# Decoder layer on one core: how the decay factors of the gated delta rule are made, and where some key, gate and selection work stands

## The chip, the cores and the metric

One core of a Trainium2 chip runs the whole layer as one program. The metric is the device time of one launch in microseconds (us). Five engines run their own instruction streams and meet at semaphores: PE (TensorE, matmuls), DVE (VectorE), ACT (ScalarE), POOL (GpSimd) and SP (SyncE, which here only issues DMAs). All arithmetic is in 32-bit floats, so the trace shows several PE records for each matmul.

## The reference

The input is x (4 x 256 x 256) and a context (4 x 256 x 64). Three things follow each other: a linear attention with state (gated delta rule with two keys and values per token, 8 heads of width 128), a mix of its output by a top-k mask over similarities of the context, and a feed-forward part with 8 routed experts. The change touches the first, and the order of the selection that belongs to the second:

```
q = conv_silu(x @ Wq), k = conv_silu(x @ Wk), v = conv_silu(x @ Wv)   (two k, v per token)
q = l2norm(q) / sqrt(Dh),  k = l2norm(k),  beta = 2 sigmoid(x @ Wb)
g = -exp(A_log) * softplus(x @ Wa + dt_bias)                           (one per token and head)
per token:  state *= exp(g);  for j in 0, 1:
                u = (v_j - k_j . state) * beta_j;  state += k_j (x) u
            o = q . state
out = (rmsnorm(o) * norm_w * silu(x @ Wg)) @ Wo
```

The kernel works through it in chunks of 64 tokens (4 per sequence, 16 in all). Within a chunk it needs, for each pair of positions, exp of a sum of g between them; across chunks exp of the sum from the start and to the end.

## The kernel before

**Steps and stages.** `run_heads` runs 11 steps (0 to 10). In step s head s is in stage A, head s-1 in B, s-2 in C and s-3 in E, so four heads are worked on side by side. Each engine has its own program with the same step loop, and each step has a place `FIRST`, slots 0 to 11 and a place `LAST`. The table `FILL` says which extra piece ("item") of which stage stands in which place; PE fills a PSUM bank with it, and another engine empties the bank. Items share three banks in rotation (`bank_of`), so PE waits for the item three before.

- Stage A: ten projections (`proj`, line 582) in slots 0 to 9 through two banks; ACT copies each with the last filter tap (`evac`, line 833), DVE adds the other three taps (`conv`, line 1055), ACT applies silu (line 857) and squares; PE sums the squares (`norm`, line 611), DVE takes them over (`norm_sum`, lines 1083 to 1091) and folds them into beta (`fold_beta`, lines 1100 to 1105).
- The decay factors of head A: POOL multiplies g by a mask of "upto" (`gm`, line 1287), PE sums it over tokens in the items `dx` and `ex` (line 596, four products of 64 x 128 x 512), ACT takes exp of each bank (line 872, after a load of the table for exp, line 866). POOL masks dx into `dm` (line 1308), later multiplies dx by minus beta (line 1315), then makes `kn` (line 1296), copies scalars and multiplies q by ex into `qE` (line 1337).
- Stage B: the items `pair` at `FIRST` (eight, line 637), which DVE empties with two products into `aT` and `mq` (lines 1121 and 1126); then the inverse of the triangular 128 x 128 matrices. For it SP writes the diagonal 32 x 32 blocks of `aT` to memory (line 445) and reads them back turned so that a block lies in a partition (`blk`, line 448), POOL solves them in 62 dependent operations (`invert`, lines 1370 and 1373), SP writes and reads back the result (lines 454 and 459, the last as four DMAs into `TT`), DVE transposes it (`turn_blocks`, slot 9, line 1144), and PE combines it in the items p32 (line 663), t32 (667), x32 (669), p64 (671) and t64 (673) with ACT copies between them. `vtok` and `kend` (line 639) are transposes of v and k; DVE scales kend (line 1132). `gate` (line 590) are the gate products, which ACT passes through silu.
- Stage C is the scan over the chunks (lines 683, 697, 711, 712, 716). After it ACT squares the output (`out_square`, line 889) and DVE makes `og` (line 1197). Stage E is the output projection `out` (line 746).

**Order.** It is written out by hand: each engine goes through its instructions in program order, and so does SP's queue. In a step SP issues gather (`a_blocks`, `blk`), the loads of weights, a tile of similarities, and scatter (the inverses). In step 1 it then writes out the similarities (`tiles_out`, line 425) and waits for them; POOL waits for the same before it clears `TT` of head 1. POOL's order in a step is: clear and unit of the inverse (lines 1347, 1354, 1358), cwh and gm, the factor of stage E, invert, dm, fold, kn, scalars, qE. DVE also works on the top-k selection: `topk` runs 20 operations for each tile, 8 in slot 0 and 12 in slot 11.

After the steps the feed-forward part follows, which the change doesn't touch.

## Time and profile before

| what | value |
|---|---|
| median of 3 runs | 939.75 us (938.98 to 943.63) |
| the profiled execution's own time | 943.89 us |
| its span, from first to last instruction | 941.8 us |
| PE busy | 834.6 us (89%) |
| DVE busy | 527.5 us (56%) |
| ACT busy | 393.7 us (42%) |
| POOL busy | 346.9 us (37%) |
| mean granted TensorE clock | 0.942 of 2.4 GHz |

The steps can be told in the trace by the eight pair items (line 637) with which each begins on PE: steps 1 to 8 begin at 55.0, 120.5, 187.8, 255, 320.8, 386.4, 453.7 and 519.7 us. DVE's transpose into X (line 1144) ends at 108.0, 170.8, 373.0 and 572.4 us in steps 1, 2, 5 and 8, and SP's first gather DMA of step 2 is issued at 123.8. The feed-forward part is from 625 us to the end. Within one engine rows that follow each other are merged; "[x <- y]" is idle time ahead of the row and what ended it.

### The profile page before, as it was taken

The numbers are of one execution on the slowest core, as the hardware profiler recorded it, in microseconds if no ns is written. First come the engines' busy times: TensorE is split into PE (matmuls) and PEld (weight loads), VectorE is DVE, ScalarE is ACT, GpSimd is POOL, SyncE is SP. The second block draws the span as 40 slices with busy tenths as digits, with TensorE's granted clock in tenths as the row PEclk, the third lists the DMA queues.
The fourth block names the chain that finished last, engine by engine and source line by source line (L and its number), as shares of the span: only waits on it lengthen the run. The fifth ranks groups of instructions, "written<-read, shape, count | busy, mean of one in ns | idle before, by whom it ended". The sixth has DMA issues, their size and how long they took to land.

```text
span 941.8 us, 16248 instructions
## 1 busy us (share of the span) xinstructions
PE 834.6 (89%) x5560; PEld 582.0 (62%) x5561; DVE 527.5 (56%) x1283; ACT 393.7 (42%) x843; POOL 346.9 (37%) x654
## 2 busy tenths in 40 slices
PE   3759999989999999899899766867999999999992
PEld 2334576766766766667667755755666667666761
DVE  4655668678878878878888763564411111111113
ACT  3637765455654565555565332113222222222220
POOL 0158358437456564573584470003420000000015
PEclk9978999799999999999999975985999999999997
DMA  8320330030031021121201301019563101110104
GB/s 203 79 59 9 74 79 13 13 79 12 13 79 23 9 73 23 35 46 24 51 2 24 90 3 26 1 33 377 194 238 111 33 22 33 33 33 22 33 24 127
DMA packets 102594, 57.88 MB, mean 61 GB/s; under 512 B 64192, under 2 KB 98048, under 8 KB 102528
## 3 DMA queue, kind: packets, MB, share of 16 engines
q1 hardware_dynamic: 99488, 51.62, 20.4%
q0 software_dynamic: 1536, 4.20, 1.5%
q10 hardware_dynamic: 1504, 1.20, 0.4%
q8 instruction: 39, 0.64, 0.3%
q14 instruction: 27, 0.22, 0.1%
HBM read 42.45 MB, written 14.55 MB: 61 GB/s over the span
## 4 chain that ended last, share of the span: by engine, by line
PE 70%; DVE 7%; POOL 7%; ACT 6%; issue 5%; DMA 4%; SPq 1%; POOLq 0%; ACTq 0%; DVEq 0%
PE bank L1600 16%; PE bank L582 11%; PE bank L1645 9%; PE bank L590 3%; PE bank L637 3%; PE bank L746 3%; DVE y L1055 3%; PE bank L712 2%; POOL inv L1373 2%; POOL term L1370 2%; PE bank L1632 2%; PE bank L711 2%; PE bank L697 2%; PE bank L596 2%; PE bank L671 2%
## 5 line engine op out<-in xcount | busy, mean ns | idle before, releaser
L1055 DVE SCALAR_TENSOR_TENSOR y<-bank,cwh,y 128x510 f32<-128x510 f32 (+2 forms) x240 | 177.5, 743 | 77.1 <-ACT y L833 73.4
L582 PE MATMUL bank<-xnT,wbuf 128*128 128x512 f32 x320 | 159.8, 624 | 7.4 <-DVE y L1055 6.8
L1600 PE MATMUL bank<-f_wgu,f_xgT 128*128 x368 | 118.8, 466 | 0.0
L1878 DVE TENSOR_TENSOR f_act<-f_sg,bank 128x352 f32<-128x352 f32 x62 | 32.2, 521 | 144.3 <-PE bank L1600 142.0
L1370 POOL TENSOR_TENSOR term<-inv,blk 128x126 f32<-128x126 f32 (+22 forms) x248 | 87.4, 352 | 62.8 <-DMA blk<-a_blocks 44.0
L1953 POOL DMA_INDIRECT f_back<-slots_y,f_slot x16 | 15.4, 960 | 231.5 <-DMA slots_y<-f_yb 224.9
L1373 POOL TENSOR_TENSOR inv<-inv,term 128x126 f32<-128x126 f32 (+22 forms) x248 | 91.1, 367 | 19.4
L582 PEld LDWEIGHTS bank<-xnT,wbuf 128*128 128x128 f32 x320 | 55.6, 193 | 66.2 <-issue 50.8
L1717 ACT ACTIVATE f_sg<-bank 128x352 f32<-128x352 f32 x62 | 28.6, 463 | 161.7 <-PE bank L1600 153.3
L1645 PE MATMUL bank<-f_wdn,f_actT 128*128 (+1 forms) x372 | 91.5, 388 | 0.9 <-ACT f_actT L1730 0.8
L1600 PEld LDWEIGHTS bank<-f_wgu,f_xgT 128*128 128x128 f32 x368 | 66.2, 190 | 36.8 <-issue 7.6
L833 ACT ACTIVATE y<-bank,cwh 128x512 f32<-128x512 f32 x80 | 54.9, 686 | 71.2 <-PE bank L582 69.3
L1645 PEld LDWEIGHTS bank<-f_wdn,f_actT 128*128 128x128 f32 x372 | 67.9, 189 | 24.5 <-issue 12.0
L1315 POOL TENSOR_TENSOR dx<-dx,minus_beta 128x1024 f32<-128x1024 f32 x8 | 15.2, 1902 | 114.6 <-DVE beta_n L1105 114.6
L637 PE MATMUL bank<-kq 128*128 128x192 f32 x256 | 46.3, 336 | 8.0 <-DVE mq L1126 8.0
L712 PE MATMUL bank<-mq,R 128*128 128x64 f32 x256 | 48.0, 286 | 3.1 <-DVE R L1162 3.1
L932 ACT ACTIVATE vtok<-bank,kn 128x128 f32<-128x128 f32 x128 | 36.4, 369 | 30.1 <-PE bank L642 30.1
L637 PEld LDWEIGHTS bank<-kq 128*128 128x128 f32 x256 | 42.2, 193 | 10.6 <-DVE mq L1126 9.8
L1300 POOL TENSOR_TENSOR factor<-factor,masks 128x8 f32<-128x8 f32 x8 | 13.3, 1662 | 88.8 <-DVE factor L1206 88.8
L1600 PE MATMUL bank<-f_wgu,f_x2T 128*128 128x352 f32 x128 | 45.5, 503 | 0.4 <-DVE f_act L1878 0.4
L712 PEld LDWEIGHTS bank<-mq,R 128*128 128x128 f32 x256 | 39.9, 203 | 6.6 <-DVE R L1162 3.7
L596 PE MATMUL bank<-gm,masks 64*128 64x512 f32 x64 | 27.5, 686 | 14.6 <-ACT dx L872 8.0
(206 smaller groups left out, 1511.7 us busy)
## 6 DMA issues: line engine op xcount, KB each, us to landing
f_wgu<-in_exp_gu SPq DMA_DIRECT2D x8, 1408.0 KB, 9.4
f_wdn<-in_exp_dn SPq DMA_DIRECT2D x8, 640.0 KB, 9.9
blk<-a_blocks SPq DMA_DIRECT2D x16, 256.0 KB, 3.8
slots_x<-oT SPq DMA_DIRECT2D x24, 128.0 KB, 1.9
f_xg<-slots_x SPq DMA_DIRECT2D x24, 128.0 KB, 2.0
slots_y<-f_yb SPq DMA_DIRECT2D x23, 128.0 KB, 1.7
a_blocks<-aT SPq DMA_DIRECT2D x64, 32.0 KB, 1.6
inverses<-inv SPq DMA_DIRECT2D x16, 128.0 KB, 3.0
```

Source lines behind the costliest of these rows:

```text
L582: last = mm(bankA[p % 2][:, :], wbuf[A.par][:, kt, wblk, :], xnT[:, kt, (p % 2) * 512:(p % 2 + 1) * 512], start=kt == 0, stop=kt == 1)
L596: return mm(bank[:, :], mask("rest" if kind == "dx" else "ones", i * STEPS, STEPS), gm[half_, :, :].rearrange("p n t -> p (n t)"), start=T ...
L637: last = mm(bank[:, c * (MU + STEPS):(c + 1) * (MU + STEPS)], kraw[:, 2 * n + c, :], kq[:, 2 * n + c, :], start=True, stop=True)
L712: last = mm(out, U[:, b, :], mq[par][:, b, c, :], start=c == 0, stop=True)
L833: a(y[p % 2][:, :, :].rearrange("p b t -> p (b t)"), bankA[p % 2][:, :], ACT.Copy, scale=cwh[A.par][:, cb, 3:4]).then_inc(evac_done, 1)
L932: last = a(vtok[B.par][:, b, c, :], bank[:, c * P:(c + 1) * P], ACT.Copy, scale=kn[:, b * CH + c:b * CH + c + 1])
L1055: v.scalar_tensor_tensor(out=y[p % 2][:, :, k:], in0=src[:, :, 0:SEQ - k], scalar=cwh[A.par][:, cb, 3 - k:4 - k], in1=y[p % 2][:, :, k:], ...
L1370: g.tensor_tensor(step_term, inv[:, 0:r, j:j + 1].to_broadcast([P, r, k]), blk[:, j:j + 1, j + 1:].to_broadcast([P, r, k]), ALU.mult).then ...
L1373: g.tensor_tensor(inv[:, 0:r, j + 1:], inv[:, 0:r, j + 1:], step_term, ALU.add).then_inc(inv_done if j == NB - 2 else inv_step, 1)
L1600: last = mm(gu[c][:, 0:FFH], xt[:, k, :], wgu[:, e, k, at:at + FFH], start=k == 0, stop=k == 1)
L1645: last = mm(dn[par][:, 0:HID], aT[0:rows, par, k, :], wdn[0:rows, e, k, :], start=k == 0, stop=k == FT - 1)
L1878: v.tensor_tensor(av[:, par, half * FFH:(half + 1) * FFH], sg[:, half, :], gu[2 * half + 1][:, 0:FFH], ALU.mult).then_inc(f_act, 1)
```

## The change

The sums of g are made once for all heads, in two small products in step 0, and kept both as columns (`g_cols`, a token pair per partition) and as rows in memory (`sums`). For each head SP loads the rows of the head into all 128 partitions, twice: into `dr` (for pairs) and into `ex`. POOL subtracts the column from the row and masks with an affine select; ACT takes exp of `dr` into `dm` and of `ex` in place, one instruction of 1024 columns each; POOL makes dx from dm and minus beta. The items dx and ex are gone from PE, and gm from POOL.

Besides: ACT scales kend (four copies with a scale) in place of DVE; kend 2 moves from slot 11 to 9, the gate products from slots 9 and `LAST` to 4 and 9; `norm(A, 5)` moves behind x32, in a new place `BLOCKS_64` ahead of `LAST`; `out_square` moves there too, ahead of p64; of the four DMAs into TT those of blocks 0 and 2 are issued first, and DVE waits for these two alone; topk is split 5, 4 and 11 operations in slots 0, 2 and 11.

```diff
 FILL = {FIRST: {"B": [("pair", n) for n in range(BC // 2)]},
-        0: {"A": [("dx", 0), ("dx", 1), ("ex", 0), ("ex", 1)]},
...
-        4: {"E": [("out", 1)]},
+        4: {"E": [("out", 1)], "B": [("gate", 0)]},
...
-        9: {"B": [("gate", 0)]},
+        9: {"B": [("kend", 2), ("gate", 1)]},
         10: {"B": [("p32", 0), ("p32", 1)], "E": [("out", 3)]},
-        11: {"B": [("t32", 0), ("t32", 1), ("kend", 2)]},
-        LAST: {"B": [("x32", 0), ("x32", 1), ("gate", 1), ("p64", 0), ("p64", 1), ("t64", 0), ("t64", 1)]}}
+        11: {"B": [("t32", 0), ("t32", 1)]},
+        BLOCKS_64: {"B": [("x32", 0), ("x32", 1)]},
+        LAST: {"B": [("p64", 0), ("p64", 1), ("t64", 0), ("t64", 1)]}}
+SCALARS_AT = 3
+EXP_AT = {0: 7, 1: 2}
```

SP's queue:

```diff
+        def rows_to(A_h, out, done):
+            for i in range(2):
+                src = halves[i][A_h * BC // 2:(A_h + 1) * BC // 2, :].rearrange("(a n) t -> a (n t)", a=1)
+                sp.dma_start(out[:, i * BC // 2:(i + 1) * BC // 2, :]..., src.to_broadcast([P, BC // 2 * STEPS])).then_inc(done, 16)
+        def difference_rows(h):
+            if h:
+                sp.wait_ge(dm_done, h)
+            rows_to(h, dr, dr_in)
+        def decay_rows(h):
+            if h:
+                sp.wait_ge(qe_done, 2 * h)
+            rows_to(h, ex, ex_in)
...
             if B:
                 gather(B)
+            if s == 1:
+                decay_rows(1)
             if A and A.h < HEADS - 1:
                 loads(A.h + 1)
...
+            if s == 0:
+                ...        (writes the rows out, waits, difference_rows(0), decay_rows(0))
+            if A and A.h < HEADS - 1:
+                difference_rows(A.h + 1)
             if B:
                 scatter(B)
+            if A and 1 <= A.h < HEADS - 1:
+                decay_rows(A.h + 1)
             if s == 1:
                 tiles_out()
                 tile_in(0)
```

ACT (per head; in steps 0 and 1 both stand in slots 7 and 2, else before slot 0 with `keep_k` between them) and POOL:

```diff
+        def decays(A):
+            nc.scalar.preload_act_table_set(LN_EXP)
+            act.wait_ge(ex_in, 32 * (A.h + 1))
+            a(ex[:, :, :], ex[:, :, :], ACT.Exp).then_inc(ex_done, 1)
+        def pair_decays(A):
+            act.wait_ge(dr_step, 2 * A.h + 2)
+            if A.h:
+                act.wait_ge(qk_used, 8 * A.h)
+            a(dm[:, :, :], dr[:, :, :], ACT.Exp).then_inc(dm_done, 1)
+        def differences(h):                                              # POOL
+            pool.wait_ge(dr_in, 32 * (h + 1))
+            g.tensor_tensor(dr, dr, g_cols[:, h, :] (broadcast), ALU.subtract).then_inc(dr_step, 1)
+            pool.wait_ge(dr_step, 2 * h + 1)
+            g.affine_select(out=dr, in_=dr, pattern=[[0, BC], [2, STEPS]], ..., fill=-1000.0).then_inc(dr_step, 1)
...
-                decays(A)
                 fold_beta(A)
                 norm(A)
                 scalars(A)
                 q_decay(A)
+                if A.h < HEADS - 1:
+                    differences(A.h + 1)
```

## Rows read from the trace of the kernel before

**Rows 1.** Busy time by stage: us, PE, PEld, DVE, ACT, POOL, PEclk, DMA share, GB/s

```profile
320.90:386.50 65.60, 62.71 (x533) 44.33 (x533) 54.49 (x127) 37.45 (x73) 38.40 (x77) 1.00 0.17 37
386.50:453.90 67.40, 64.50 (x533) 45.04 (x534) 54.60 (x127) 37.50 (x74) 38.47 (x77) 0.97 0.18 37
```

**Rows 2.** Timeline of step 5 (320 to 386 us): start us, us, engine, line

```profile
320.77 2.22 PE L637 MATMUL bank<-kq 128*128 128x192 f32 x12
324.33 3.52 PE L637 MATMUL bank<-kq 128*128 128x192 f32 x20 [1.33 <-DVE mq L1126]
334.51 0.69 ACT L833 ACTIVATE y<-bank,cwh 128x512 f32<-128x512 f32 x1 [1.32 <-PE bank L582]
371.57 1.42 DVE L1144 STREAM_TRANSPOSE X<-TT 32x512 f32<-32x512 f32 x2
373.38 1.20 PE L663 MATMUL bank<-X,aT 32*32 32x32 f32 x64
380.33 1.07 ACT L946 ACTIVATE XP<-bank 64x512 f32<-64x512 f32 x2
382.52 2.08 PE L671 MATMUL bank<-XP,aT 64*64 64x64 f32 x32
```

**Rows 3.** Groups of instructions by line: busy us, mean ns, idle before

```profile
L596 PE MATMUL bank<-gm,masks 64*128 64x512 f32 x64 | 27.5, 686 | 14.6 <-ACT dx L872 8.0 <-POOL gm L1287 6.6
L639 PE MATMUL bank<-masks,kT 128*128 128x128 f32 x96 | 16.2, 296 | 0.0
L1132 DVE TENSOR_TENSOR kend<-bank,sh 128x512 f32<-128x512 f32 x24 | 16.4, 684 | 10.5 <-PE bank L639 10.5
L932 ACT ACTIVATE vtok<-bank,kn 128x128 f32<-128x128 f32 x128 | 36.4, 369 | 30.1 <-PE bank L642 30.1
L1315 POOL TENSOR_TENSOR dx<-dx,minus_beta 128x1024 f32<-128x1024 f32 x8 | 15.2, 1902 | 114.6 <-DVE beta_n L1105 114.6
L889 ACT ACTIVATE osq<-oT 128x1024 f32<-128x1024 f32 x8 | 8.4, 1045 | 0.0
```

**Rows 4.** Chain of waits of step 2, from the last product into aT

```profile
125.99 0.44 DVE aT L1121
...
170.08 0.70 DVE X L1144
```

**Rows 5.** DVE and POOL at the ends of steps 1 and 5, and line 1358

```profile
114.49 1.01 DVE L1091 TENSOR_SCALAR qn<-turned 128x8 f32<-128x8 f32 x1
...
383.82 2.50 POOL L1337 TENSOR_TENSOR qE<-kq,ex 128x512 f32<-128x512 f32 x2
...
385.75 1.53 DVE L1091 TENSOR_SCALAR qn<-turned 128x8 f32<-128x8 f32 x1
...
388.09 1.28 DVE L1197 SCALAR_TENSOR_TENSOR og<-oT,normw,gate 128x1024 f32<-128x1024 f32 x1 [0.82 <-ACT osq L889]
389.29 0.42 DVE L1121 TENSOR_TENSOR aT<-bank,dx 128x256 f32<-128x256 f32 x1
...
L1358 POOL TENSOR_SCALAR_AFFINE_SELECT inv<-inv x16: 716/722/1772, 64.6 to 521.4; 64x512 f32<-64x512 f32 x16
```

**Rows 6.** Timeline of step 0 (ACT) and of the start of step 1 (PE)

```profile
28.10 1.28 ACT L866 ACT_TABLE_LOAD   x1 [1.47 <-PE bank L596]
...
67.52 3.75 PE L596 MATMUL bank<-gm,masks 64*128 64x512 f32 x6 [6.13 <-POOL gm L1287]
```

**Rows 7.** Timeline of step 1: SP's queue, and POOL's qE

```profile
104.19 7.71 SPq L425 DMA_DIRECT2D similarities<-TT  x4
...
118.61 2.50 POOL L1337 TENSOR_TENSOR qE<-kq,ex 128x512 f32<-128x512 f32 x2
```

**Rows 8.** Timeline of the end of step 8, and DMAs by line

```profile
584.49 3.78 PE L590 MATMUL bank<-xnT,wg 128*128 128x512 f32 x4
...
594.33 0.64 PE L725 MATMUL bank<-osq,masks 128*32 128x256 f32 x8 [1.63 <-ACT osq L889]
...
blk<-a_blocks SPq DMA_DIRECT2D x16, 256.0 KB, 3.8
```

More of the change, by code:

```diff
@@ L144, in order_table @@
         for place in PLACES:
-            for stage, items in items_at(place, step):
+            for stage, items in items_at(place):
                 if 0 <= step - LAG[stage] < HEADS:
@@ L752, in fill @@
             def fill(place):
-                for stage, items in items_at(place, number(A, B, C, E)):
+                for stage, items in items_at(place):
                     if stages[stage]:
@@ L819, in scalar_values @@
             for i in range(2):
+                a(g_rows[0:HEADS * BC // 2, i * STEPS:(i + 1) * STEPS], bankC[i][0:HEADS * BC // 2, 256:256 + STEPS],
+                  ACT.Copy).then_inc(rows_done, 1)
+            for i in range(2):
                 v = bankC[i][:, 0:256].rearrange("p (i h n) -> p i h n", i=4, h=HEADS)
@@ L914, in item @@
         def item(kind, n, B):
-            if kind not in ("vtok", "p32", "t32", "x32", "p64", "t64", "dx", "ex", "gate"):
+            if kind not in ("vtok", "p32", "t32", "x32", "p64", "t64", "kend", "gate"):
                 return
@@ L918, in item @@
             bank = bankB[bank_of(kind, B.h, n)]
-            if kind in ("dx", "ex"):
-                decays(B, kind, n, bank)
+            if kind == "kend":
+                if n == 0:
+                    act.wait_ge(sh_done, B.h + 1)
+                if B.h:
+                    act.wait_ge(s_mm, 3 * (B.h - 1) + n + 1)
+                for b in range(BATCH):
+                    at = b * CH + n
+                    last = a(kend[:, b, n, :], bank[:, b * P:(b + 1) * P], ACT.Copy, scale=sh[B.par][:, 1, at:at + 1])
+                last.then_inc(kend_done, 1)
                 return
@@ L968, in fill @@
             def fill(place):
-                for stage, items in items_at(place, number(A, B, C, E)):
+                for stage, items in items_at(place):
                     if stages[stage]:
@@ L983, in step @@
                 fill(slot)
-                if s == 0 and slot == FIRST_DECAYS:
+                if s == 0 and slot == SCALARS_AT:
                     scalar_values()
+                if slot == EXP_AT.get(s, -1):
+                    decays(A)
+                    pair_decays(A)
                 if s == 1 and slot < 11:
@@ L1107, in item @@
         def item(kind, n, B):
-            b = n
-            if kind not in ("pair", "kend", "out"):
+            if kind not in ("pair", "out"):
                 return
@@ L1221, in fill @@
             def fill(place):
-                for stage, items in items_at(place, number(A, B, C, E)):
+                for stage, items in items_at(place):
                     if stages[stage]:
@@ L1243, in step @@
                 if tiles and slot == 0:
-                    topk(tiles[0], 0, 8)
+                    topk(tiles[0], 0, 5 if A else 8)
+                if A and tiles and slot == 2:
+                    topk(tiles[0], 5, 9)
                 if not A and tiles and slot == 5:
```

158 lines of the change are left out of this document (79 added, 79 removed).

## The prediction

> **What bounds the kernel now.** I read the table of steps first, then the timeline of one full step, the chain of waits, and last the groups by line. In a full step PE is busy 62.7 of 65.6 us [rows 1]: PE sets the pace, and what is taken from it counts. The second thing to see is how close the next limit is. The inverse of the 32 x 32 blocks comes back through POOL and three memory trips; DVE turns it until 371.57 + 1.42 = 372.99, and PE starts p32 at 373.38 [rows 2]. So PE finds it ready by only 0.4 us. Whatever shortens PE ahead of p32 by more than that meets the inverse.
>
> The loop of the inverse is: last product into aT, blocks out and back, 62 operations on POOL, out and back, transpose. In step 2 it ran with nothing late, from 125.99 + 0.44 = 126.43 to 170.08 + 0.70 = 170.78, 44.35 us [rows 4]. To close the loop one adds the eight pair items on DVE and the time from X's end to the first of them, which in step 5 was 389.29 - 372.99 = 16.3 us [rows 2, 5].
>
> **Steady steps, PE's side.** The items dx and ex go: 27.5 / 8 = 3.4 us a head, and the wait for ACT inside them, 8.0 / 8 = 1.0 [rows 3]: -4.4. Ahead of p32 come gate 1 (3.78 at the half clock is 1.9 at full [rows 8]) and kend 2 (16.2 / 24 = 0.7 [rows 3]): +2.6; gate 0 only changes its slot. The old way from the first pair to p32 is 373.38 - 320.77 = 52.6; the new one 50.8, or 49.5 if the wait of 1.33 in the pairs [rows 2] goes too. Behind p32 the old tail, to the next step, is 65.6 - 52.6 = 13.0. There kend 2 only filled a wait for ACT, so I count nothing. Gate 1 stood between x32 and p64; without it p64 waits for the first copy of XP, ready near 380.33 + 0.6, so it starts some 1.5 before 382.52 [rows 2]. PE alone could do a step in 50.8 + 11.5 = 62.3, at best 49.5 + 11.5 = 61.
>
> **Steady steps, the loop of the inverse.** Two of four DMAs into TT no longer count. SP issued the four in about 1.9 us, so this is worth about 1.0 (below by 0 if the landing, and not the issue, is last): 44.35 - 1.0 = 43.4. The pairs take DVE 4.8. Between X and the pairs DVE loses kend 2 (0.68 [rows 3]), one operation of topk (about 0.5), and the wait of 0.82 for ACT's square [rows 5], since that square now stands ahead of p64: 16.3 - 2.0 = 14.3. Against it stands POOL. It now runs the subtraction (1.9, the nearest row being the product with minus beta [rows 3]) straight behind qE, and og, which reads two tiles of SBUF, falls among them: +0.3 as I read the two timetables, between -1.3 (nothing blocks) and +2.2 (og behind the subtraction). That is 14.6 + 4.8 + 43.4 = 62.8 us a step, and this is above PE's 62.3: the loop takes over. Bounds 61 and 65.
>
> Six laps run from X of step 2 to X of step 8. They took 572.4 - 170.8 = 401.6 in all, 66.9 each, among other things because some steps ran a stretch at 1.2 GHz: 67.4 us at a mean clock of 0.97 against 65.6 at 1.00 [rows 1]. New: 6 x 62.8 = 376.8, and 3 for such stretches: 380. Gain 22.
>
> **Covers.** kend on ACT is 12 copies of 0.37 [rows 3], 4.4 us a head, beside PE and DVE; ACT is busy 37.5 of 65.6 [rows 1]. If that cover were gone, it would be 4.4 a step. POOL loses dm and gm, gets the subtraction and an affine select (716 ns for 512 columns [rows 5], so about 1.4): both end before blk has landed. ACT's two exps of 1024 columns cost about 1.05 each, as the square of 1024 does [rows 3]; four of 512 go. The first copy of a step, at 334.51 - 320.77 = 13.7 in the old one [rows 2], now waits for: qE's end (1.7 into the step), issue and landing of the rows (1.0 + 3.8, as blk [rows 8]), exp, keep_k of 2.2, exp: 10.8. PE doesn't need it before about 12.
>
> **The opening.** Step 0: rows out and in, and two more table loads (28.10, 1.28 each [rows 6]) in a phase where ACT has half a microsecond to spare per slot: +2.5 (0 to 5). In sentences that the sum can do without: the Trainium skill ("ScalarE: Activation LUTs", What ACT_TABLE_LOAD costs) puts a drain of 1.38 us behind each load, 2.66 together. In the trace the next ACT instruction starts 1.29 after the load's start, so the row decides; by the page it would be +5.3.
>
> Step 1: PE's stall of 6.1 for gm and the slow products behind it (67.52 to 73.5 [rows 6]) vanish. Eleven microseconds of PE, but the inverse of head 0 sits behind it: DVE turned it at 106.5, two microseconds before p32, and that time doesn't move except by the 1.0 of TT. So step 1 gives 2 to 3 only, the same as step 0 takes.
>
> Step 2 pays for a queue. `decay_rows(2)` stands in SP's queue ahead of `tiles_out`, and waits for both qE of head 1, which end at 118.61 + 2.50 = 121.1 [rows 7]; the similarities went out at 104.19 before. Behind it: rows 1.0, four DMAs of 256 KB about 5, the wait for them, then tile_in, and only then gather of head 1, which it had at 123.8. I get 128, 4.4 us late, and it enters the loop in full: X of step 2 ends near 173.7 instead of 170.8 (bounds 168 and 177). Cost 2.9.
>
> **The close.** In step 8 the gate products of 3.78 and the wait of 1.63 for the square [rows 8] go, both on the path behind p32: 3.5 + 1.6 = 5.1. Behind step 8 nothing changes.
>
> **Sum.** The profiled execution: 943.9 + 2.9 - 22 - 5.1 = 919.7. It stands 4.1 above the median of the runs (943.89 against 939.75), so the median after is about 916.
>
> **Rivals.**
> (a) *The lock between DVE and POOL.* qn, 0.17 us when free, took 1.53 at 385.75: it ended 0.96 after qE had ended at 386.32, behind POOL's two memsets; at 114.49 it got in directly when the product with minus beta ended [rows 5]. For it: five steps show 1.53. Against: in the one boundary of two products qn wins. If og or qn stays behind the subtraction, the way from X to the pairs is 16.5 and the lap 64.7: six laps 388.2 + 3, gain 10.4, which gives 943.9 + 2.9 - 10.4 - 5.1 = 931.3, median 927. The Trainium skill ("SBUF — State Buffer", Who interferes with whom) says that a DVE instruction with two SBUF inputs blocks fully against a GpSimd instruction that reads SBUF, for the whole instruction; by that rule this is what happens, and which of the two comes first decides the size. Chance 0.2.
> (b) *PE's best.* og slips in, the loop has slack, the queue of step 1 costs nothing: 6 x 61 = 366, gain 36, and 5.1: 903, median 899. Against it: the 0.4 us ahead of p32. Chance 0.16.
> (c) *Slower: ACT held at the head of each step by `ex_in`.* ACT executes in order, and the exp of ex stands ahead of keep_k, of the first copy and so of all filter taps. From a landing 2.9 us later than I count (13.7 against 10.8), 6.7 after the issue, each further microsecond is one a step; only the shorter tail of 1.5 is left on the other side. With the 2.9 and 5.1 of opening and close it turns slower than before at 6.7 + 1.5 + 0.3 = 8.5. Rows read by 128 partitions from one place are shown nowhere in the trace. At 10 us: 943.9 + 7 x (3.3 - 1.5) + 2.9 - 5.1 = 954, median 950. The gather behind these rows in SP's queue adds to it. Chance 0.11.
> (d) *It evens out:* (a) and a late opening, 939. Chance 0.08.
> My forecast has 0.45.
>
> **Chances.** This kernel's runs tell 0.5% (4.7 us) from no change: 935.1 to 944.5. Faster: 0.45, (b) 0.16, (a) 0.19 of its 0.2: 0.80. Same: 0.09. Slower 0.11. The range: the forecast's own is 908 to 924; with (b)'s 899 and (a) with a late opening it is 899 to 936, which leaves out (c), (d) and what is below (b).
>
> **What would show it.** No line like 596 on PE; the distance of the pair items 62 to 63.5 us (61 for b, 65 for a); the first transpose into X ended by a DMA and PE idle before p32 because of DVE; qn and og on DVE against the subtraction on POOL; in step 1 SP's write of the similarities behind 121 and gather of step 2 near 128; the landing of the rows below 5 us. I am wrong if ACT's idle time ahead of the exps is ended by these DMAs with more than 3 us, or if p32 still finds its inverse ready.

## The result, and the profile after

| | before | after |
|---|---|---|
| median | 944.26 us (938.98 to 947.90, 10 runs) | 929.50 us (925.25 to 935.42, 10 runs) |
| ratio, 95% interval | | 0.985 (0.982 to 0.9885) |
| profiled execution | 943.89 us, span 941.8 | 929.86 us, span 928.1 |
| mean granted clock | 0.942 | 0.920 |

The changed kernel is 1.5% faster. Ratios and intervals here and below compare the fast runs of both kernels, those within 1.5% of a kernel's fastest. I had forecast 919.7 against the profiled execution, 24.2 us of gain, and it came to 14.0. For the median I had taken off another 4.1 us, because three runs had a median of 939.75; ten have 944.26, so the profiled execution was a typical one and nothing was to be taken off. The granted clock is given as a share of 2.4 GHz: 1.00 is 2.4, 0.50 is 1.2, and a number between is the mean of stretches at these two.

Steps 5 and 6 by stage, as [rows 1], in the kernel after (us, then PE, PEld, DVE, ACT and POOL busy, PEclk, DMA):

```profile
317.99:381.51 63.52, 61.30 (x526) 45.22 (x524) 54.87 (x124) 40.51 (x83) 39.73 (x78) 0.97 0.27 55
381.51:444.07 62.56, 60.91 (x525) 45.14 (x524) 51.93 (x124) 40.72 (x83) 36.60 (x76) 0.98 0.24 56
```

65.6 and 67.4 have become 63.5 and 62.6. The timeline of step 5, after, answers to [rows 2]:

```profile
317.99 2.22 PE L674 MATMUL bank<-kq 128*128 128x192 f32 x12
320.85 3.52 PE L674 MATMUL bank<-kq 128*128 128x192 f32 x20 [0.64 <-DVE mq L1186]
366.64 1.43 DVE L1196 STREAM_TRANSPOSE X<-TT 32x512 f32<-32x512 f32 x2 [1.18 <-DMA TT<-inverses]
368.21 1.20 PE L702 MATMUL bank<-X,aT 32*32 32x32 f32 x64 [0.52 <-DVE X L1196]
375.90 2.14 PE L710 MATMUL bank<-XP,aT 64*64 64x64 f32 x32 [0.37 <-ACT XP L1000]
```

Before, PE came to p32 (the first product behind the inverse) with the inverse ready. Now PE waits for X, and X waits for its DMA: the loop of the inverse has taken over, as forecast. From the first pair to p32 it is 50.2 us (forecast 50.8), from p32 to p64 7.7 (9.1 before).

What I had priced too low is in the column of the granted clock (PEclk). Windows from p32 to the next step's first pair, which I call the tail, in the kernel before (steps 2 and 5; in step 8 to the end of t64):

```profile
170.92:187.84 16.92, 16.83 (x249) 13.66 (x249) 10.34 (x29) 8.79 (x18) 11.08 (x12) 0.70 0.01 1
373.38:386.41 13.03, 13.03 (x253) 11.02 (x252) 11.66 (x31) 8.70 (x18) 7.62 (x7) 1.00 0.01 3
572.59:592.69 20.10, 20.10 (x236) 16.32 (x236) 2.14 (x4) 6.93 (x15) 0.00 (x0) 0.58 0.03 7
```

and after (steps 1, 2, 4, 5, 7 and 8):

```profile
110.29:124.99 14.70, 14.66 (x229) 12.62 (x229) 4.14 (x10) 8.14 (x17) 10.46 (x8) 0.54 0.09 26
177.14:194.10 16.96, 16.96 (x240) 15.66 (x241) 13.15 (x28) 9.25 (x18) 12.25 (x10) 0.50 0.17 33
306.30:317.99 11.69, 11.06 (x244) 9.94 (x245) 10.84 (x30) 9.04 (x18) 6.34 (x6) 1.00 0.01 3
368.21:381.51 13.30, 12.66 (x244) 11.53 (x244) 12.45 (x30) 9.05 (x18) 7.95 (x7) 0.86 0.01 2
494.91:508.20 13.29, 12.66 (x244) 11.59 (x245) 12.44 (x30) 9.05 (x18) 7.94 (x8) 0.84 0.02 4
561.77:579.47 17.70, 17.60 (x232) 16.63 (x236) 2.73 (x4) 7.29 (x15) 0.00 (x0) 0.50 0.03 9
```

Nearly the same tail takes 11.69 us at 2.4 GHz (step 4) and 16.96 at 1.2 (step 2). In steps 3 to 7 the kernel before has 1.00 five times, and 1.00 and 0.70 in steps 1 and 2; the one after has 1.00 in three of the five, and 0.54 and 0.50 in steps 1 and 2.

Where the 14.0 us come from, by the prediction's own parts:

| part | forecast | measured |
|---|---|---|
| step 0, to the first pair | +2.5 | 59.84 - 54.98 = +4.9 |
| step 1, first pair to X | step 1 in all -2 to -3 | 50.30 - 52.98 = -2.7 |
| step 1, X to the next first pair | | 14.85 - 12.53 = +2.3 |
| step 2, first pair to X (the queue) | +2.9 | 52.00 - 50.28 = +1.7 |
| X of step 2 to X of step 8 | -22 | 384.63 - 401.66 = -17.0 |
| X of step 8 to the end of og | -5.1 | 48.9 - 52.1 = -3.2 |
| the rest | 0 | 0.0 |

### The profile page after: what moved, and what is told of

Same layout as the page of the kernel before. It is cut to its first block and busy times, and to the rows that moved or that the text cites. A ratio compares the mean times of both kernels' runs of the same rounds, so it can differ in the third digit from the quotient of the medians.

```text
span 928.1 us, 16187 instructions
## 1 busy us (share of the span) xinstructions
PE 824.0 (89%) x5500; PEld 593.7 (64%) x5501; DVE 518.9 (56%) x1259; ACT 421.4 (45%) x929; POOL 344.9 (37%) x654
## 5 line engine op out<-in xcount | busy, mean ns | idle before, releaser
L1656 PEld LDWEIGHTS bank<-f_wgu,f_xgT 128*128 128x128 f32 x368 | 66.2, 190 | 36.8 <-issue 7.6
L1366 POOL TENSOR_TENSOR dx<-dm,minus_beta 128x1024 f32<-128x1024 f32 x8 | 15.2, 1902 | 107.7 <-issue 91.9
L674 PE MATMUL bank<-kq 128*128 128x192 f32 x256 | 52.0, 367 | 1.9 <-DVE mq L1186 1.9
L674 PEld LDWEIGHTS bank<-kq 128*128 128x128 f32 x256 | 48.8, 218 | 3.7 <-DVE mq L1186 2.8
L1346 POOL TENSOR_TENSOR factor<-factor,masks 128x8 f32<-128x8 f32 x8 | 13.3, 1664 | 72.4 <-DVE factor L1258 72.4
L1946 DVE COPY f_yb<-bank 128x256 f32<-128x256 f32 x23 | 9.8, 425 | 53.0 <-PE bank L1701 53.0
```

The lines of the kernel that those rows point to most:

```text
L674: last = mm(bank[:, c * (MU + STEPS):(c + 1) * (MU + STEPS)], kraw[:, 2 * n + c, :], kq[:, 2 * n + c, :], start=True, stop=True)
L1656: last = mm(gu[c][:, 0:FFH], xt[:, k, :], wgu[:, e, k, at:at + FFH], start=k == 0, stop=k == 1)
```

## The experiments

Each variant was run beside the kernel before on one chip; a ratio is to that kernel, with its 95% interval. The changed kernel has 0.985 (0.982 to 0.9885), and on the chip of the variants with two fillers 0.988 (0.984 to 0.993). Single variants can therefore be told apart by their ratios only from about 0.8% on; most verdicts rest on the traces, of which there is one for each variant.

### The first group: four suspects

**Gate product back into the tail.**

```diff
-        9: {"B": [("kend", 2), ("gate", 1)]},
+        9: {"B": [("kend", 2)]},
...
-        BLOCKS_64: {"B": [("x32", 0), ("x32", 1)]},
+        BLOCKS_64: {"B": [("x32", 0), ("x32", 1), ("gate", 1)]},
```

> The changed kernel with gate product 1 taken out of slot 9 and put back between x32 and p64. Theory (the clock): in the changed kernel the short products behind p32 run at the granted clock of 1.2 GHz in steps 1, 2 and 8, because PE had waited for X ahead of p32 and nothing wide follows; the 512-column gate product between x32 and p64 brings 2.4 GHz back, so p64 and t64 (3.3 us each) fall to about 1.65 each, and the pairs behind them (2.3 for six) to about 1.4. In steps 1, 2 and 8 that pays for the product (3.8 at the half clock against 3.3 + 1 to 2): about 0 there; in the five other steps the product costs 1.9 less what it hides of the wait for the first copy of XP (up to 1.5): +0.4 each. Sum +2, and the ratio to the kernel before 0.985 to 0.988. Rival (the path only, no clock): p64 and t64 stay at 3.3 in steps 1, 2 and 8, and each of the eight steps grows by 0.4 to 1.9: +9 to +15, a ratio of 0.995 to 1.0.

Measured: ratio 1.007 (1.002 to 1.011), 20 us worse than the changed kernel by the ratios, and neither theory had it. In this trace steps 3 to 6 have all lost the clock (steps 3 and 4 shown):

```profile
247.68:266.64 18.96, 18.96 (x248) 14.93 (x249) 11.82 (x30) 9.73 (x19) 12.42 (x12) 0.64 0.09 29
315.38:334.18 18.80, 18.80 (x249) 14.70 (x249) 12.19 (x30) 9.84 (x19) 12.65 (x12) 0.64 0.09 30
...
315.38 1.20 PE L702 MATMUL bank<-X,aT 32*32 32x32 f32 x64 [1.72 <-DVE X L1196]
325.87 3.78 PE L636 MATMUL bank<-xnT,wg 128*128 128x512 f32 x4
```

X came 1.5 us earlier after the first pair (48.9 in the mean of steps 3 to 7, against 50.3), since the pairs were through in 5.47 us instead of 6.4 to 6.9. But PE, without the 1.9 us of the product, came to p32 earlier still: the wait became 1.6 to 2.4 us instead of 0.3 to 1.0, and behind that wait the products as far as the gate product ran at half speed (step 7, with a wait of 1.61, kept its clock). So here a product in slot 9, where it fills the wait, is worth more than its time.

**SP's queue.** The write of the similarities and its reading back moved ahead of `decay_rows(2)`:

```diff
-            if A and 1 <= A.h < HEADS - 1:
-                decay_rows(A.h + 1)
             if s == 1:
                 tiles_out()
                 tile_in(0)
+            if A and 1 <= A.h < HEADS - 1:
+                decay_rows(A.h + 1)
```

> The changed kernel with one order changed in SP's queue: in step 1 the write and reading back of the similarities stand ahead of the rows of ex for head 2. Theory (queue): the write goes out at about 110 instead of 122.8, gather of step 2 is issued at about the first pair + 3.4 us (it was + 6.9), and X of step 2 comes 3 to 4 us earlier against the first pair; PE then waits less than 0.5 us ahead of p32 there instead of 3.79, and if that keeps the clock up, x32, p64 and t64 of step 2 take 5 us less too. Gain 3 to 8 us: a ratio to the kernel before of 0.977 to 0.982. Rival (the cost of the opening is in step 0 and step 1, on ACT and POOL, and the queue is hidden): X of step 2 moves by less than 1 us, ratio 0.984 to 0.986.

Measured: 0.988 (0.981 to 0.995), nothing to be told by time. In the trace the write is issued at 112.46, the first gather DMA of step 2 at the first pair + 5.0 (before + 3.4, after + 6.9), and the first pair to X's end takes 50.65 instead of 52.00. The queue is real and costs 1.4 us, where I had expected 3 to 4; PE still waits 3.78 ahead of p32 and not less than 0.5, and the tail stays at 0.51.

The rows of it in the changed kernel, from rows of ex to gather, stand in the order in which I had put them, gather 8 us later than before:

```profile
121.94 0.81 SPq L463 DMA_DIRECT2D ex<-sums  x2
122.80 2.25 SPq L432 DMA_DIRECT2D similarities<-TT  x4
131.46 0.33 SPq L426 DMA_DIRECT2D simw<-similarities  x1
131.84 3.88 SPq L452 DMA_DIRECT2D a_blocks<-aT  x8
```

**Fillers.** Products of 512 columns that nobody reads, into p32's bank ahead of its wait:

```diff
+FILLERS = {0: 1, 1: 4}
...
+            def some_mm(k):
+                for i in range(k):
+                    mm(bank[:, :], wg[h % 2][:, 0, :], xnT[:, 0, 0:512], start=True, stop=True)
+            if h in FILLERS:
+                some_mm(FILLERS[h])
+            if h == HEADS - 1:
+                some_mm(2)
+                pe.wait_ge(inv_out, 32 * (h + 1))
+                some_mm(2)
...
+            if kind == "p32" and n == 0:
+                fillers(h, bank)
             if kind == "p32":
```

> The changed kernel with products of 512 columns that nobody reads ahead of p32's wait for X (into p32's bank, which p32 then overwrites): one in step 1, four in step 2, four in step 8 (two of these behind the write of the inverses). Theory (the clock): they keep the granted clock at 2.4 GHz through X's arrival, so the tail from p32 to the next step's first pair falls from 14.7 to about 12 in step 1 and from 17.0 to 11.7 in step 2, and in step 8 the way from X's end to the end of t64 from 17.9 to about 12. Together 10 to 14 us less: a ratio to the kernel before of 0.970 to 0.975. Rival (the clock falls for another reason than the wait, or the products come too early to hold it): the tails stay as they are, and the ratio is 0.985 (up to 0.988 if the fillers run into X's arrival).

Measured: 0.986 (0.980 to 0.9925). Step 2 did what the clock theory says. With the fillers, and without them in the changed kernel:

```profile
173.59 3.60 PE L660 MATMUL bank<-xnT,wg 128*128 128x512 f32 x8
177.27 1.20 PE L718 MATMUL bank<-X,aT 32*32 32x32 f32 x64
...
188.26 2.06 PE L688 MATMUL bank<-kq 128*128 128x192 f32 x11
```

```profile
177.14 1.92 PE L702 MATMUL bank<-X,aT 32*32 32x32 f32 x64 [3.79 <-DVE X L1196]
187.45 3.35 PE L710 MATMUL bank<-XP,aT 64*64 64x64 f32 x29
```

Work that nobody reads makes the tail 11.0 us instead of 17.0. In step 1 the clock held until p64 and then fell all the same (0.72 in the mean), though PE had no wait left ahead of p32: p64 and t64 took 3.3 us each. In step 8 the four fillers ended 3.8 us ahead of X, and the tail stayed at 0.50 and 17.7 us. The ratio can't be told from the changed kernel's.

**Head 0 without the table loads.** It leaves out head 0's decays.

```diff
-            nc.scalar.preload_act_table_set(LN_EXP)
+            if A.h:
+                nc.scalar.preload_act_table_set(LN_EXP)
...
-            a(ex[:, :, :], ex[:, :, :], ACT.Exp).then_inc(ex_done, 1)
+            a(ex[:, :, :], ex[:, :, :], ACT.Exp if A.h else ACT.Copy, scale=1.0 if A.h else 0.0).then_inc(ex_done, 1)
```

> The changed kernel with the two exps of head 0 in step 0 turned into copies (scale 0) and without the load of the table ahead of them; the load behind them goes too. It leaves out head 0's decays. Theory (opening): of the 4.9 us by which the first pair of step 1 comes later than in the kernel before, the two loads (1.28 each) are 2.6 and the rest is the wait for the rows and the exps themselves, as long as copies; so the first pair comes about 2.6 us earlier (57.2 instead of 59.8), and the loop carries this to the end: a ratio of 0.982. Rival (the rows' landing through POOL sets the place, and the loads are hidden beneath it): the first pair moves by less than 0.7, ratio 0.985.

Measured: 0.987 (0.981 to 0.992), first pair at 57.5. The start of a run moves by some 4 us from one execution to the next, so I count from the first load of the silu table. To the first pair it is then 36.9 us in the changed kernel, 35.0 to 38.3 and in the mean 36.8 in the sixteen profiles of all variants with the same step 0, and 31.3 without the two loads (the kernel before: 32.4). So 2.6 us of loads cost 5.5, by one profile against the mean of sixteen; without them step 0 is as short as in the kernel before, and the rows' way out and in costs nothing there. The changed kernel, and then this variant:

```profile
45.55 1.28 ACT L902 ACT_TABLE_LOAD   x1
...
48.04 0.65 PE L651 MATMUL bank<-osq,masks 128*32 128x128 f32 x8 [4.19 <-ACT osq L929]
48.62 3.78 PE L628 MATMUL bank<-xnT,wbuf 128*128 128x512 f32 x4
```

```profile
47.47 0.43 PE L651 MATMUL bank<-osq,masks 128*32 128x128 f32 x8 [0.87 <-ACT osq L930]
47.83 1.98 PE L628 MATMUL bank<-xnT,wbuf 128*128 128x512 f32 x4
```

The loads turn a wait of PE of 0.9 us into one of 4.2, and the projection behind it runs at half speed. That the +5.3 named in the prediction comes near the 5.5 is luck: no drain stands behind the loads, the next operation starts 1.29 behind the start of the load.

### The second group: the lock and the size of the wait

**POOL's subtraction early** (`differences(h + 1)` moved ahead of `fold_beta`, from head 1 on):

> The changed kernel with the subtraction and the affine select for the next head put ahead of the product with minus beta on POOL (from step 1 on; in step 0 as before), where POOL waits 12 to 14 us for DVE anyway. Theory (the lock of rival a): og takes 2.36 us instead of 1.28 because it runs against the subtraction; with nothing but memsets there it takes 1.28 again, the subtraction 1.90, the pairs' products on DVE start 1.1 us earlier against X, and the steady laps fall from 61.7 to 62.5 to about 61: five laps, 4 to 6 us, a ratio to the kernel before of 0.979 to 0.981. Rival (the laps are held by PE and by its clock, not by DVE): og is short, but the distance of the pair items stays within 0.3 us of 61.7, a ratio of 0.985.

Measured: 0.9865 (0.982 to 0.991), and og still takes 2.36: my culprit was the wrong one. In the changed kernel og starts inside the second product of qE (until 319.18) and ends 1.08 us behind it; the subtraction is in turn held by og (2.88 instead of 1.90). DVE goes from og straight to the first product into aT:

```profile
316.69 2.49 POOL L1388 TENSOR_TENSOR qE<-kq,ex 128x512 f32<-128x512 f32 x2
317.90 2.36 DVE L1249 SCALAR_TENSOR_TENSOR og<-oT,normw,gate 128x1024 f32<-128x1024 f32 x1
319.14 2.88 POOL L1353 TENSOR_TENSOR dr<-dr,g_sums 128x1024 f32<-128x1024 f32 x1
320.19 0.41 DVE L1181 TENSOR_TENSOR aT<-bank,dx 128x256 f32<-128x256 f32 x1
```

**qE first** (`q_decay(A)` moved ahead of `fold_beta(A)` on POOL), run with the third group:

> The changed kernel with the two products of qE put ahead of the product with minus beta on POOL, where POOL waits for DVE. Theory (the lock is with qE, as the variant with the subtraction moved showed: og starts 1.1 to 1.3 us before the second product of qE ends, and waits for it): og takes 1.28 us in steps 3 to 7, the last product into aT ends 1.1 us earlier after the first pair, the way from the first pair to X's end falls from a mean of 50.2 in steps 3 to 7 to about 49.3, and the rows of ex go out 6 us earlier, so ACT's wait for them ends. Laps -0.9, where PE has the same to give (it waits 0.3 to 1.0 for X): 4 to 5 us, ratio to the kernel before 0.980 to 0.982. Rival (PE's way from the first pair to p32 is the same length, so nothing comes of it): og short, X no earlier than 0.3, ratio 0.985.

Measured: 0.990 (0.985 to 0.994). og is free of the lock (step 5),

```profile
312.40 2.50 POOL L1388 TENSOR_TENSOR qE<-kq,ex 128x512 f32<-128x512 f32 x2 [12.14 <-PE bank L751]
320.31 1.90 POOL L1353 TENSOR_TENSOR dr<-dr,g_sums 128x1024 f32<-128x1024 f32 x1
322.16 1.27 DVE L1249 SCALAR_TENSOR_TENSOR og<-oT,normw,gate 128x1024 f32<-128x1024 f32 x1
```

and the first pair to X's end is no shorter (50.6 to 51.6 in steps 3 to 7, against 49.8 to 50.7). But this does not show that the lock is free. In steps 3 to 6 the pairs ran at a clock of 0.69 to 0.75 (changed kernel: 0.80, 1.00, 1.00, 0.78). In step 7, the one with pairs at 1.00, the lock had only moved: qn, 0.17 us when free, now takes 1.63 against the subtraction, og and the first product into aT stand behind it, and PE waits 1.70 in the pairs:

```profile
451.35 1.90 POOL L1353 TENSOR_TENSOR dr<-dr,g_sums 128x1024 f32<-128x1024 f32 x1
451.65 1.63 DVE L1153 TENSOR_SCALAR qn<-turned 128x8 f32<-128x8 f32 x1
454.39 0.41 DVE L1181 TENSOR_TENSOR aT<-bank,dx 128x256 f32<-128x256 f32 x1
```

The two variants of the rebuilt tail below don't settle it either: with og at 2.36 the way is 48.7 to 50.2, with og at 1.27 and, in three steps, qn at 1.63 it is 48.9 to 50.6. So the lock exists and costs og 1.1 us. In the changed kernel this lies on the loop: in steps 4, 5 and 7 the first product into aT starts 2.19 us behind the first pair, as soon as og is through, and PE waits 0.64 in the pairs. What a kernel without the lock would gain no variant shows; from these rows I estimate up to 1 us a lap. The Trainium skill ("SBUF — State Buffer", SBUF: two separate sides) has the shared ports as an exclusive lock, which goes to whoever of the two starts first, for the whole instruction, also for a DVE operation with two SBUF inputs against a GpSimd operation that reads SBUF. The trace agrees, with 1.1 us for og and 1.0 for the subtraction.

**All four blocks of TT before X** (the old order of the four DMAs, and X waits for `tt_in` and `tt_odd`):

> The changed kernel with the two halves of the DMAs into TT undone: X waits for all four blocks, issued in the old order. Theory (X's loop bounds, my 44.4 against 43.4 us): the wait for the DMA ahead of X grows by about 1.0 us in every step, PE waits 1.3 to 2 instead of 0.3 to 1.0 ahead of p32, and that is the wait behind which the clock fell in the variant with gate product 1 moved back; so the laps grow by 1.0 at least and by up to 6 where the clock falls: +8 to +35 us, ratio 0.994 to 1.02. Rival (the landing of a block and not its issue is last, or DVE comes late to X anyway): within 0.3 a lap, ratio 0.985 to 0.987.

Measured: 0.9996 (0.996 to 1.003), 14 us worse. From the first pair to X's end all eight steps grow, by 0.1 to 2.0 us, 1.06 in the mean: my 1.0 for the halved landing was right. That is 8.4 us. In the profiles 5.3 more are tails that lost the clock (step 5: 17.9 us at 0.53 behind a wait of 1.75; step 6: 13.3), and 1.7 stand ahead of the first pair.

**Fillers in each step:**

> The changed kernel with unread 512-column products on PE: ahead of p32 one in each step, four in step 2 and eight in step 8, and one ahead of p64 in steps 1 and 8. Theory (the clock): the granted clock stays at 2.4 GHz behind p32 in steps 1, 2 and 8, where it fell in the changed kernel; tails: step 1 from 14.7 to 12.5, step 2 from 17.0 to 11.7 (as four fillers alone gave), step 8 from 17.9 between X's end and t64's end to 12.5. The fillers in the steady steps fill waits of 0.3 to 1.0 us and cost up to 0.6 each. Sum -10: 919.5, a ratio to the kernel before of 0.972 to 0.977, and the mean granted clock near 0.94. Rival (step 8's clock falls whatever PE does, since nothing of a next head runs there): only step 2's 5 us: 0.980 to 0.984.

Measured: 0.979 (0.975 to 0.983), between the two theories. Step 8 went from 17.9 to 16.2, not to 12.5, and steps 3, 5 and 7 still had 0.77 to 0.83, with next to no wait ahead of p32. **Three together** (early subtraction, queue, fillers) did no better:

> The changed kernel with three things together: the subtraction ahead of the product with minus beta on POOL, the similarities ahead of the rows for head 2 in SP's queue, and fillers ahead of p32 (one in step 1, three in step 2, eight in step 8) and ahead of p64 (one in steps 1 and 8). By my theory the gains add: 5 for og, 1.4 for the queue (X of step 2 against the first pair, 50.6 to 49.2), 10 for the clock: 929.5 - 16 = 913, a ratio to the kernel before of 0.966 to 0.970. Rival (they are one gain taken twice, since an earlier X needs no filler and PE bounds the laps at 61.7): 918 to 920, a ratio of 0.973 to 0.975.

Measured: 0.984 (0.979 to 0.989). Neither the sum of the gains nor the rival's number. Its profile has 0.82, 0.82, 0.77, 1.00 and 0.55 in the tails of steps 3 to 7, the first two without a wait ahead of p32; the gain in step 2 (a tail of 12.9 us) stands against losses there.

### The third group: the tail rebuilt

**Gate product in the tail, output item and fillers ahead of p32.** To the first group's move of gate 1 it adds

```diff
-        10: {"B": [("p32", 0), ("p32", 1)], "E": [("out", 3)]},
+        10: {"E": [("out", 3)], "B": [("p32", 0), ("p32", 1)]},
```

and one filler in each step, four in step 2, eight in step 8.

> The changed kernel with gate product 1 back between x32 and p64, the last item of the output product (1.13 us) moved from behind p32 to ahead of it, and unread 512-column products ahead of p32 (one in each step, four in step 2, eight in step 8). Theory (the clock has two conditions: no wait of more than about a microsecond ahead of p32, and a wide product in the tail): the granted clock from p32 to the next step's first pair is 1.00 in steps 2 to 7, as in the kernel before, where the changed kernel has 0.50 to 1.00 and the variant with only the gate product moved back 0.64; tails of 12.3 to 13.0 us in each, laps of 62 to 63; 922 us, ratio 0.973 to 0.978. Rival (the long tails of that variant are the gate product's own and not the clock's): tails of 14 or more at whatever clock, ratio 0.99 to 1.0.

Measured: 0.984 (0.980 to 0.987): the clock is 1.00 in steps 2, 3, 4 and 7 (tails of 12.5 to 12.8), but 0.78 and 0.88 in steps 5 and 6, where one filler left waits of 1.04 and 1.57 (step 7 kept it with 1.43). The rival's tails of 14 or more did not come in those four, but neither did the theory's 0.973 to 0.978; and the profile is of the fastest of six executions (924.3 us, median 929.8), so it shows the clock at its best. With qE first and the queue added:

> The variant with the tail rebuilt (gate product 1 in the tail, the output product's last item and unread products ahead of p32), with qE's products first on POOL and the similarities first in SP's queue. By my theory their gains add: og 1.28, laps 61.5, X of step 2 1.4 us earlier against its first pair: 915 us, ratio 0.966 to 0.971. Rival (PE bounds the laps once it has the gate product in the tail and the fillers ahead of p32): as without them, 0.973 to 0.978.

Measured: 0.986 (0.982 to 0.990); no gain from the two. Here too the profile is of the fastest execution (922.7, median 933.0).

**The kernel before, with its gate product taken out of the tail** (`("gate", 1)` from `LAST` to slot 9):

> The kernel before with one edit: gate product 1 moved from between x32 and p64 to slot 9, behind gate product 0. It tests the clock from the other side: PE then comes to p32 1.9 us behind X and waits for nothing there. Theory (a tail of narrow products alone loses the clock in part of the steps, even without a wait): the granted clock from p32 to the next first pair, 1.00 in six of eight steps, falls below 0.9 in two or more of steps 2 to 7; each such tail is 1.6 to 5 us longer; the other laps grow by 0.4 or less: ratio 1.005 to 1.02. Rival (only the wait ahead of p32 costs the clock): the tails keep 1.00, their time falls from 13.4 to about 12 and the way to p32 grows by 1.9: ratio 1.000 to 1.004.

Measured: 0.9994 (0.997 to 1.002), and the rival holds in steps 2 to 7: tails of narrow products alone, all at full clock, when PE comes late to p32. Step 2, which had 0.70 behind a wait of 1.18, has 1.00 without one. But step 1, at 1.00 in the kernel before, has 0.77 with no wait. Steps 3 and 4:

```profile
245.03:256.57 11.54, 11.16 (x250) 10.34 (x249) 10.31 (x28) 8.10 (x17) 6.14 (x5) 1.00 0.01 3
310.90:322.45 11.55, 11.16 (x250) 10.34 (x249) 10.32 (x28) 8.11 (x17) 6.14 (x5) 1.00 0.01 3
```

**With two fillers and without any.** The rebuilt tail and the queue's order in both; one has two unread products ahead of p32 in each step (six in step 2, seven in step 8), the other none.

> The changed kernel with gate product 1 back between x32 and p64, the output product's last item ahead of p32, the similarities first in SP's queue, and unread products of 512 columns ahead of p32: two (1.9 us) in each step, six in step 2, seven in step 8. Theory (a wait ahead of p32 takes the clock, a wide product in the tail keeps it): PE waits for X less than 0.7 us in every step, the granted clock from p32 to the next first pair is 0.95 to 1.00 in steps 2 to 7, tails of 12.6 to 13.2, laps of 61.5 to 62.5; 918 us, a ratio to the kernel before of 0.970 to 0.976. Rival (the clock falls in part of the tails whatever PE does ahead of p32): two or more tails of steps 3 to 7 below 0.9 with waits below 0.7, ratio 0.98 to 0.985.

> The variant with two fillers without any filler: PE waits for X ahead of p32, about 1 to 2 us in steps 3 to 7, 5 in step 2, 7 in step 8. Theory (the wait): the clock in the tails of steps 3 to 7 is 0.64 to 0.7 in most of them, tails of 15 to 18, laps of 65 to 68, and the whole is 20 us or more slower than with the unread products: ratio 0.995 to 1.01. Rival (fillers only cost their time): the tails stay at 0.9 or above, the laps at 62 or below, and it is as fast as with fillers or up to 5 us faster: 0.965 to 0.975.

Measured, on one chip: 0.975 (0.971 to 0.980) with them, 0.991 (0.988 to 0.995) without: unread work makes the kernel 15 us faster. Both theories of the first are half right: the ratio is the one forecast, but two of the steady tails have 0.88 with waits below 0.2, and step 2 has 0.77 (the profile is of the slowest execution, 927.0 us). Steps 3, 4 and 5 with fillers (no wait ahead of p32), then without (waits of 0.87, 1.23 and 1.07):

```profile
245.27:257.59 12.32, 12.05 (x245) 9.86 (x244) 11.47 (x29) 9.53 (x19) 7.79 (x7) 1.00 0.01 3
307.13:319.45 12.32, 12.05 (x245) 9.85 (x245) 11.47 (x29) 9.54 (x19) 7.63 (x7) 1.00 0.01 3
369.06:383.46 14.40, 13.82 (x244) 10.68 (x244) 12.80 (x30) 9.63 (x19) 9.05 (x7) 0.88 0.03 9
```

```profile
241.62:258.23 16.61, 16.52 (x245) 12.74 (x245) 12.55 (x30) 9.82 (x19) 11.12 (x8) 0.69 0.14 27
307.34:323.96 16.62, 16.53 (x245) 13.44 (x245) 12.55 (x30) 9.72 (x19) 11.13 (x8) 0.69 0.08 27
372.92:388.33 15.41, 15.10 (x244) 11.52 (x244) 13.23 (x30) 9.73 (x19) 9.92 (x8) 0.78 0.08 19
```

On the same chip the kernel with two fillers beats the changed one too:

> The changed kernel itself again, beside the three variants on the same chip. Both theories expect its ratio of 0.982 to 0.9885; its profile is to show whether the same tails lose the clock again: by the theory of the wait steps 1, 2 and 8 always (waits of 1.3, 3.8 and 7.4 us), the steady steps (waits of 0.3 to 1.0) now one and now another; by its rival (a property of each step's work) the same steady steps, 5 and 7, as in its first profile.

Measured: 0.988 (0.984 to 0.993). In its profile steps 1, 2 and 8 have lost the clock again (0.63, 0.50, 0.50), step 1 this time without any wait ahead of p32; of the steady ones step 6 (0.84), where the first profile had steps 5 and 7. So it changes from one execution to the next.

**Narrow tail with two fillers:**

> As the variant with two fillers, but gate product 1 stays in slot 9 (so the tail holds narrow products only; five fillers in step 2). Both theories have PE at p32 behind X. Theory (the wait decides alone, as the kernel before without its gate product in the tail suggests): clock 0.95 to 1.00 in the tails of steps 3 to 7, tails of 10.7 to 11.8 but p32 up to 1.5 behind X, laps of 62 to 63, ratio 0.972 to 0.978. Rival (a narrow tail falls without a wait, as with one filler: 0.77 to 0.83 in half the tails): two or more tails of steps 3 to 7 at 0.7 to 0.9, laps of 63 to 65, ratio 0.980 to 0.988.

Measured: 0.981 (0.978 to 0.984). No waits, yet 0.83, 0.83 and 0.82 in steps 5 to 7: the rival.

### The fourth group: step 0

> The variant with two fillers, with four more unread products of 512 columns in step 0, ahead of the norm product of slot 8 where PE waited 4.2 us behind the table loads, and with three ahead of p32 in step 1 (two before) and eight in step 2 (six before). Theory (the loads' 2.6 us turned into 6.5 by the clock): the projection behind that wait takes 1.98 us and not 3.78, and the way from the first load of the silu table to the first pair falls from 37.8 (mean of four profiles) to about 35.5; with the tails of steps 1 and 2 at 2.4 GHz too, 3 to 6 us less than the variant with two fillers: ratio 0.968 to 0.973. Rival (step 0 is held by ACT's queue, whatever PE's clock): 37.8 stays within 0.7, ratio as the variant with two fillers.

> The variant with two fillers again, on the same chip as the one with fillers in step 0. Expected by its first runs: a ratio to the kernel before of 0.971 to 0.980.

Measured: with fillers in step 0 and more in steps 1 and 2, 0.971 (0.963 to 0.979), but its eight runs spread from 910 to 928 us with a median of 924.8, and the interval rests on the lowest four of them; the variant with two fillers beside it had a median of 923.7 and 0.984 (0.978 to 0.989), outside the 0.971 to 0.980 that I had expected of it again. I take this as no difference. In the trace the projection behind the loads takes 1.98 us instead of 3.78, and the way to the first pair 35.1 us, as the theory says; but in the profile of the variant without those fillers it is 35.0 too (its projection took 3.00). In the tails step 2 has 1.00, but step 1, with three fillers and no wait, 0.66 and 17.5 us: that part of the theory failed. One execution each can't tell it; the clock in step 0 also falls in some executions and less in others.

## Why the prediction was off

**Right.** The loop of the inverse takes over from PE, by 0.3 to 1.0 us. The four laps from X of step 3 to X of step 7 take 61.67, 61.92, 64.16 and 62.53, in the mean 62.6; I had 62.8. This is in part luck: the two laps with nothing lost are 1 us shorter than my sum, and a lost clock makes up the difference. kend on ACT costs nothing (96 copies of 370 ns, in the place of [rows 3]'s 684 ns on DVE). Rival (c) did not come: rows of 256 KB land in 4.5 us, and the first copy of y comes 10.1 us after the first pair (forecast 10.8). The sign that I had set for it did come, since ACT waits 4.1, 4.2 and 4.3 us for the rows in steps 4, 5 and 7; it was badly chosen, for my own sum of 10.8 has that wait in it. The early blocks of TT are worth 1.06 (forecast 1.0). The queue in step 1 is there, at 1.4 to 1.7 us (forecast 2.9). Rival (a)'s lock is there too, with qE and not with the subtraction; its price is open.

**The step that failed** is the term "and 3 for such stretches", for stretches at 1.2 GHz in the six laps, and that opening and close had no such term at all. I took the clock's loss as a constant of the kernel, carried over from [rows 1], when it depends, at least in step 2, on how long PE waits, and the change moves the waits. A second step failed beside it: I took the lap of step 8 to be like the others. By the parts of the table:

- Laps: 384.6 us, where I had 6 x 62.8 + 3 = 379.8, so 4.8 more. A lap with nothing lost in its tail takes 11.84 + 50.34 = 62.2 (from X's end to the first pair, and from there to X's end in the mean of steps 3 to 7); six of them are 3.7 less than forecast. The tails that lost the clock add 8.5 (5.3 in step 2, 1.6 each in steps 5 and 7): 5.5 more than the 3 allowed. By the same count the kernel before lost 3.6, all in step 2. And X of step 8 comes 53.4 us after the first pair, 3.1 more than the mean of steps 3 to 7. That is not the clock. Without a stage A DVE has the whole top-k of a tile in slot 9 ahead of X there, and goes to X straight from it, 5.4 us behind the issue of the second DMA into TT, where steps 3 to 7 have 2.3 to 2.6:

```profile
554.45 1.93 SPq L487 DMA_DIRECT2D TT<-inverses  x4
560.11 0.15 DVE L1130 COPY thr<-m 128x1 f32<-128x1 f32 x1
560.19 1.43 DVE L1196 STREAM_TRANSPOSE X<-TT 32x512 f32<-32x512 f32 x2
```

The top-k stood there in the kernel before too, but X waited for all four DMAs and started 2.6 us behind the issue of the last, so little of it showed.

- Opening: step 0 takes 2.4 more than forecast. The loads' 1.28 each were read rightly from [rows 6], but they stand on ACT's path to PE, PE waited 4.2 and its next projection took 3.78. Step 1 takes 2.1 more: its tail is 2.3 longer than before, at 0.54 where the kernel before had 1.00. Against these, 1.2 less for the queue. 3.3 us together.
- Close: the gate product of [rows 8] is gone from the path of step 8, but p64 and t64 run at half speed to the end (3.35 and 3.30); in the kernel before, the clock had risen behind the product, slow itself, and t64 took 2.04. 1.9 us. In the variant with the rebuilt tail and both orders, where step 8 kept 1.00, X's end to t64's end is 12.8 us instead of 17.9.

4.8 + 3.3 + 1.9 = 10.0 of the 10.2 us. That the clock is the cause in step 2 and in step 8 is shown: fillers without use gave 11.0 for 17.0 us in step 2, and 15 us in all between two variants. That it is the whole of step 0's is likely, not shown. For step 1 the loss is there, but PE's wait is not its cause, as the next paragraph says. That the top-k holds X of step 8 is read from the trace (DVE goes from one to the other without a gap, in all twenty profiles); no variant moves it.

**What takes the clock.** Over all twenty profiles, the tails of steps 3 to 7 by PE's wait ahead of p32:

| wait ahead of p32 | tails | at 1.00 | mean | lowest |
|---|---|---|---|---|
| below 0.5 us | 54 | 31 | 0.92 | 0.74 |
| 0.5 to 1.0 | 19 | 9 | 0.91 | 0.69 |
| over 1.0 | 27 | 7 | 0.78 | 0.53 |

and in step 2 ten profiles with a wait of 3.4 us or more have 0.50 to 0.64, all ten. So a long wait goes with a lost clock, and taking it away in step 2 gave the clock back; but it is not all. Of the tails with less than 0.5 us, all ten of the kernel before and its variant have 1.00, and of the 44 of the changed kernel and its variants only 21. And in step 1 all profiles but that of the kernel before lost the clock (0.54 to 0.88), ten of these nineteen with no wait at all ahead of p32. So something else costs the clock too, more often in the changed kernel, and what it is stays open. Nor is it settled whether the wide product in the tail helps: with two fillers and the product there, the tails had 1.00, 1.00, 0.88, 1.00, 0.88 and again 1.00, 0.88, 0.69, 1.00, 0.78; without it 1.00, 1.00, 0.83, 0.83, 0.82; and the kernel before has five times 1.00 both with and without it.

**The best version** is the one with two fillers: 0.975 and 0.984 on two chips, against 0.985 and 0.988 for the changed kernel. On the chip that ran both, the intervals (0.971 to 0.980, 0.984 to 0.993) do not meet.

## What to carry to other kernels

When a change shortens an engine's work ahead of a wait that does not move, price the wait itself: here only 7 of 27 tails behind a wait of over 1 us on PE kept the full clock, a lost one cost up to 6 us, and unread wide products in the wait won 15 us against the same kernel without them, 12 against the changed one. A term for lost clock is not a constant to be carried over from the profile before; ask for each step where PE will now stand idle. Before you multiply a lap by six, look at each step that is built differently (here step 8, with no stage A). When a variant removes a lock, look where it went before you call it harmless. And take an offset between the profiled execution and the median only from more than three runs.

## What was not expected of the hardware

- A tail of 244 products took 11.69 us at a granted clock of 1.00 and 16.96 (240 products) at 0.50; the same code got 1.00 in one execution and 0.84 in the next (step 6 of the changed kernel).
- A DVE operation with two SBUF tiles that starts inside a POOL product waits to that product's end (og, 2.36 against 1.28 us), then goes ahead of POOL's next product and holds that one (the subtraction, 2.88 against 1.90).
- Rows read from one place in memory by all 128 partitions, 256 KB, landed in 4.4 to 4.5 us, hardly more than the 3.9 of `blk`, which has that size too.
